# Graph transformer layer on 4096 nodes: the first q and all of k made once for all heads and placed by DMA, the next tile's q at step 11, VectorE's LayerNorm 2 in eight parts

## The reference

```python
qkv = layer_norm(x, g1, be1) @ w_qkv                  # (N, 3, 8, 16)
scores = jnp.einsum('nhd,mhd->hnm', q, k) * SCALE
scores = jnp.where(mask, scores, -jnp.inf)            # mask = adj != 0, for all heads
attn = jax.nn.softmax(scores, axis=-1)
out = jnp.einsum('hnm,mhd->nhd', attn, v).reshape(n, DIM)
x = x + out @ w_proj + b_proj
h2 = layer_norm(x, g2, be2)
return x + gelu(h2 @ w1 + b1) @ w2 + b2
```

## Time and profile before

| | us |
|---|---|
| median of 3 runs | 1702.24 |
| lowest and highest | 1699.94, 1702.98 |
| the profiled execution | 1704.14 |
| its span | 1702.3 |

### The profile page before, as it was taken

How to read it: one execution, slowest core, us unless ns; L and a number is a source line. 1 busy time by engine, 2 the same in 40 slices (tenths; PEclk the granted TensorE clock), 3 DMA queues, 4 the chain that set the end, 5 groups by cost and what they waited for, 6 DMA issues and landing times.

```text
span 1702.3 us, 46524 instructions
## 1 busy us (share of the span) xinstructions
PE 1588.7 (93%) x17016; PEld 496.5 (29%) x17016; DVE 1419.3 (83%) x4490; ACT 1274.2 (75%) x1394; POOL 1167.4 (69%) x1092
## 2 busy tenths in 40 slices
PE   6989999999999999999999999999999999999996
PEld 3422222323223232232323232232323232232323
DVE  6888989987999889997898879998899879988811
ACT  4647878777777878778776877778787787868793
POOL 4955487569865798568875698567885688657551
PEclk9979999999999999999999999999999999999997
DMA  8810046301460046500462025700464015600000
GB/s 214 184 52 2 5 142 128 76 5 57 141 124 30 5 116 138 97 5 26 137 127 63 5 81 136 134 2 5 133 130 88 4 39 148 123 18 5 14 5 13
DMA packets 177856, 125.88 MB, mean 74 GB/s; under 512 B 140974, under 2 KB 155183, under 8 KB 177628
## 3 DMA queue, kind: packets, MB, share of 16 engines
q1 hardware_dynamic: 163196, 108.49, 26.7%
q10 hardware_dynamic: 14432, 14.42, 3.3%
HBM read 77.25 MB, written 6.04 MB: 49 GB/s over the span
## 4 chain that ended last, share of the span: by engine, by line
PE 52%; ACT 22%; issue 14%; POOL 8%; DVE 2%; ACTq 1%; DMA 1%; SPq 0%; POOLq 0%; DVEq 0%
ACT probs L820 20%; PE pv_ps L1149 15%; PE ring_ps L1080 10%; PE score_ps L1241 9%; PE score_ps L1256 9%; POOL probs L582 2%; PE ring_ps L1207 2%; PE score_ps L1173 2%; POOL k_stack L543 2%; ACT q_stack L689 1%; DVE masked_out L858 1%; PE ring_ps L1198 1%; PE ring_ps L1183 1%; PE ring_ps L1190 1%; POOL row_mask L517 1%
## 5 line engine op out<-in xcount | busy, mean ns | idle before, releaser
L858 DVE CUSTOM_DVE_ANT_0 masked_out<-ring_ps,row_mask 128x512 bf16<-128x512 f32 x2048 | 1311.9, 688 | 138.6 <-PE ring_ps L1080 99.3
L820 ACT ACTIVATE probs<-score_ps,score_scale 128x1024 f32<-128x1024 f32 x1010 | 1075.6, 1112 | 338.5 <-PE score_ps L1256 324.4
L582 POOL TENSOR_TENSOR probs<-probs,keep 128x1024 int32<-128x1024 int32 x256 | 604.2, 2361 | 252.1 <-ACT probs L820 241.6
L1149 PE MATMUL pv_ps<-probs,v_ones 128*17 128x512 f32 x4096 | 543.7, 599 | 4.6 <-POOL probs L582 4.0
L1080 PE MATMUL ring_ps<-k_stack,q_stack 51*64 51x512 f16 x4096 | 488.0, 397 | 15.1 <-DVE row_max L858 13.8
L1256 PE MATMUL score_ps<-q_stack,k_stack 51*64 51x512 f16 x4040 | 370.4, 391 | 18.9
L1080 PEld LDWEIGHTS ring_ps<-k_stack,q_stack 51*64 51x64 f16 x4096 | 169.0, 104 | 495.7 <-DVE row_max L858 446.2
L1241 PE MATMUL score_ps<-mask_t,ident_bf 64*64 64x512 bf16 x3028 | 274.9, 387 | 34.1 <-ACT probs L820 15.5
L1256 PEld LDWEIGHTS score_ps<-q_stack,k_stack 51*64 51x64 f16 x4040 | 115.6, 104 | 211.6 <-PE score_ps L1241 183.6
L858 DVE DVE_READ_ACCUMULATOR2_ANT row_max<- 128x1 f32 x2048 | 169.9, 83 | 0.0
L521 POOL TENSOR_SCALAR row_mask<-row_mask 128x1024 bf16<-128x1024 bf16 x124 | 129.5, 1045 | 23.6 <-POOL row_mask L517 23.0
(11 more groups left out here) (128 smaller groups left out, 840.3 us busy)
## 6 DMA issues: line engine op xcount, KB each, us to landing
adj_in<-adj SPq DMA_DIRECT2D x128, 512.0 KB, 4.2
halves<-attn ACTq DMA_DIRECT2D x30, 128.0 KB, 2.7
q_stack<-q_dram SPq DMA_DIRECT2D x42, 64.0 KB
mask_t<-row_mask SPq DMA_TRANSPOSE x128, 3.5
xq<-xnT_dram ACTq DMA_DIRECT2D x8, 256.0 KB, 2.7
halves<-halves ACTq DMA_DIRECT2D x16, 128.0 KB, 2.2
x_res<-x ACTq DMA_DIRECT2D x8, 256.0 KB, 4.5
out<-rows ACTq DMA_DIRECT2D x8, 256.0 KB, 5.4
```

What stands on the lines that cost most here:

```text
L582: nc.gpsimd.tensor_tensor(view, view, keep[:, KEPT.index(m), :].unsqueeze(1).broadcast_to([128, 2, TILE]), ALU.mult).then_inc(probs_masked, 1)
L820: nc.scalar.activation(probs[:, (2 * g + n) % SLOTS, :], score_banks(i, place).rearrange("p a n -> p (a n)"), ACT.Exp, scale=score_scale[: ...
L858: nc.vector.tensor_tensor_reduce(out=masked_out[:, place % 3, :], in0=ring_ps[:, place % 3, :], in1=row_mask[:, j, ch * 512:(ch + 1) * 512 ...
L1149: last = nc.tensor.matmul(pv_ps[32 * k:32 * k + HD + 1, :], v_ones[:, block_of(g, b), 2 * p + a, :], probs[:, (2 * g + b) % SLOTS, a * TIL ...
```

## The change

Three things change.

**The opening's items.** There are 9 items (`ITEMS = 1 + CHUNKS`): one for the first q and one for each chunk of k, each for all heads with the plain weight (`wq_all`, `wk_all`). ScalarE copies an item as f16 and as f32 (`take_item`), GpSimd subtracts them into the low part, ScalarE stores both parts to `item_dram` (`store_item`), and when they have landed places them: six loads for q, nine for each chunk of k (`load_item`). The replicated weights and `part_coef` go. The shift unit of k_stack is set by VectorE and spread by two DMAs. The row units run 8 steps behind instead of 7, and wait for the loads. GpSimd converts two mask pieces after each item from 1 to 6.

**q at step 11.** The fill moves from step 33, GpSimd's subtraction to step 12. SyncE stores and places q before the next tile's mask loads instead of among them.

**LayerNorm 2.** VectorE's four parts become eight, behind the second and the fourth row maximum of steps 9 to 12.

```diff
-ACT_FILLS = {H2T_STEP: ("h2t",), 33: ("q",)}
+Q_MADE = 11
+ACT_FILLS = {H2T_STEP: ("h2t",), Q_MADE: ("q",)}
-Q_STEP = 34
+Q_STEP = Q_MADE + 1
-ITEMS = PAIRS * (1 + CHUNKS)
+FIRST_PER = 4
+ITEMS = 1 + CHUNKS
-ROW_LAG = 7
+ROW_LAG = 8
-POOL_FIRST_MASKS = {4 + 2 * k: 4 + k for k in range(CONVERTED - 4)}
+POOL_FIRST_MASKS = {n: (2 * n + 2, 2 * n + 3) for n in range(1, 7)}
@@ SyncE, a tile
+                store_q(i, par)
+                load_q(i, par)
                 for k in range(CONVERTED):
                     sp.wait_ge(flag_done, (i + 1) * CONVERTED + (k - 5))
                     load_adj((i + 1) * SUB + k // ADJ_C, k % ADJ_C, k % 2)
-                    if k == Q_STORE_LOAD:
-                        store_q(i, par)
-                    if k == Q_STORE_LOAD + 1:
-                        load_q(i, par)
@@ GpSimd, the opening
-                nc.gpsimd.tensor_tensor(dst, item_x[n % DEPTH], item_neg[n % DEPTH], ALU.add).then_inc(item_done, 1)
+                nc.gpsimd.tensor_tensor(item_part[n % DEPTH][1], item_x[n % DEPTH], item_part[n % DEPTH][0],
+                                        ALU.subtract).then_inc(item_done, 1)
@@ ScalarE, the opening
+            def take_item(n):
+                act.wait_ge(item_full, n + 1)
+                if n >= DEPTH:
+                    act.wait_ge(item_stored[n - DEPTH], 32)
+                nc.scalar.copy(item_part[n % DEPTH][0], score_ps[:, n % 4, :])
+                nc.scalar.copy(item_x[n % DEPTH], score_ps[:, n % 4, :]).then_inc(item_read, 1)
+            def store_item(n):
+                act.wait_ge(item_done, n + 1)
+                for low in range(2):
+                    act.dma_start(item_dram[n, low], item_part[n % DEPTH][low]).then_inc(item_stored[n], 16)
+            def load_item(n):
+                act.wait_ge(item_stored[n], 32)
+                for m, first in enumerate(PART_ROW):
+                    low = Q_LOW[m] if n == 0 else K_LOW[m]
+                    heads = item_dram[n, low].rearrange("(p a d) n -> a d p n", a=2, d=HD)
+                    for a in range(2):
+                        rows = slice(HALF * a + first, HALF * a + first + HD)
+                        to = q_stack[0][rows, :, :] if n == 0 else k_stack[rows, :, n - 1, K_FIRST:]
+                        act.dma_start(to, heads[a]).then_inc(item_in[n], 16)
+                    if n > 0:
+                        act.dma_start(k_stack[rows, :, n - 1, 0:K_FIRST],
+                                      heads[1][:, :, 128 * 2 + 64:128 * 3]).then_inc(item_in[n], 16)
+            for c in range(CHUNKS):
+                transposed_rows(c)
+                if c == 1:
+                    load_item(0)
+                if c >= 1:
+                    load_item(c)
+                if c + 1 < CHUNKS:
+                    root(c + 1)
+                if c == 0:
+                    take_item(0)
+                take_item(c + 1)
+                act.wait_ge(stage_full, 2 * c + 2)
+                nc.scalar.copy(v_ones[:, c * SUB:(c + 1) * SUB, :, 0:HD],
+                               pv_ps[:, :].rearrange("p (s h d) -> p s h d", s=SUB, h=HEADS)).then_inc(v_done, 1)
+                if c == 0:
+                    store_item(0)
+                store_item(c + 1)
+            load_item(CHUNKS)
@@ TensorE, the opening
+                    if j == 0:
+                        pe.wait_ge(item_in[ch + 1], 16 * (3 * len(PART_ROW)))
@@ VectorE, LayerNorm 2
-                        if x == 1 and d and LN2_STEP <= g < LN2_STEP + 4:
-                            layer_norm2(i, bcd, g - LN2_STEP)
+                        if x % 2 == 1 and d and LN2_STEP <= g < LN2_STEP + 4:
+                            layer_norm2(i, bcd, 2 * (g - LN2_STEP) + x // 2)
```

More of the change, by code:

```diff
@@ L252, in program @@
         zero_dram = nc.dram_tensor("zero_dram", (SHIFT_PARTS + 1, PAIRS, TILE), F16, kind="Internal").ap()
+        item_dram = nc.dram_tensor("item_dram", (ITEMS, 2, DIM, 512), F16, kind="Internal").ap()
         q_dram = nc.dram_tensor("q_dram", (2, 2, DIM, TILE), F16, kind="Internal").ap()
@@ L328, in program @@
         item_full, item_read, item_done = sem("item_full"), sem("item_read"), sem("item_done")
+        item_stored, item_in = ([sem(f"item_stored{n}") for n in range(ITEMS)], [sem(f"item_in{n}") for n in range(ITEMS)])
+        unit_in = sem("unit_in")
         shift_full, shift_stored = sem("shift_full"), sem("shift_stored")
@@ L706, in _ @@
+            act.wait_ge(unit_set, 2)
+            for a in range(2):
+                own = k_stack[HALF * a + SHIFT_ROW:HALF * a + SHIFT_ROW + SHIFT_PARTS + 1, :, :, :]\
+                    .rearrange("r p c k -> r (p c) k")
+                act.dma_start(own[:, 1:, :], own[:, 0:1, :].broadcast_to([SHIFT_PARTS + 1, PAIRS * CHUNKS - 1, K_CHUNK]))\
+                  .then_inc(unit_in, 16)
             root(0)
-            act.wait_ge(q_clear, 2)
+            act.wait_ge(q_clear, 4)
             act.wait_ge(w_in, 16 * 5)
-            act.wait_ge(consts_in, 16 * 4)
+            act.wait_ge(consts_in, 16 * 3)
@@ L979, in layer_norm2 @@
                 before = (i - 1) * LN2_STEPS
[L980 to L985 removed]
+                if k < SUB:
+                    dve.wait_ge(row_taken, made(ROWS, i, bcd, DVE_PLACE[PROJ_STEP + k // 2]))
+                    nc.vector.bn_stats(stats[:, k, :], x_res[:, k, :]).then_inc(ln2_step, 1)
+                elif k < SUB + 2:
                     dve.wait_ge(ln2_step, before + SUB)
[L987 removed]
+                    for s in range(2 * (k - SUB), 2 * (k - SUB) + 2):
                         nc.vector.bn_aggr(mean_var[:, s, :], stats[:, s, :]).then_inc(ln2_step, 1)
[L989 removed]
+                elif k == SUB + 2:
                     dve.wait_ge(ln2_step, before + 2 * SUB)
@@ L1289, in constants @@
 def constants():
-    c = np.zeros((128, 136), np.float32)
+    c = np.zeros((128, 132), np.float32)
     c[:, 0:128] = np.eye(128)
@@ L1293, in constants @@
         c[32 * k + HD, 128 + k] = 1.0
-    for r in range(128):
-        for n, first in enumerate(PART_ROW):
-            if first <= r % HALF < first + HD:
-                c[r, 132] = -Q_LOW[n]
-                c[r, 133] = -K_LOW[n]
-        if SHIFT_ROW <= r % HALF < SHIFT_ROW + SHIFT_PARTS:
-            c[r, 135] = SHIFT_UNIT
     return c
```

103 lines of the change are left out of this document (33 added, 70 removed).

## The result

| | before | after |
|---|---|---|
| median of the runs, us | 1702.05 (4 runs) | 1725.37 (4 runs, 1723.67 to 1726.86) |
| ratio, 95% interval | | 1.0138, 1.0121 to 1.0156 |
| span of the profiled execution | 1702.3 | 1725.0 |
| first exponential of the main loop | 119.6 | 149.1 |
| from there to the end | 1582.7 | 1575.8 |

The kernel is 23.3 us slower where +9.4 was forecast. The loss is in the opening, +29.5 us; the tiles give 6.9 back, near the forecast 6.3.

What follows compares the result with a forecast made beforehand. It took GpSimd and TensorE to bound the opening, then VectorE's row maxima, and TensorE the tiles except steps 9 to 13 (VectorE). +15.7 - 5.3 - 1.0 = +9.4 us gave 1711.6 us, range 1697 to 1726.

Steps and rivals of the forecast that it cites:

- The sign: Whole kernel: forecast slower, +9.4 us; slower by over 0.2% was given 0.69.
- the tiles' sum: Eight main-loop tiles: q at step 11 and the finer LayerNorm 2 together take off 6.3 us.
- the opening's term: Opening: the DRAM chain puts the last item in place at 114.6 instead of 98.89 us, +15.7 us.
- the start: Opening: xnT's store issued by 27.3 us, then fifteen loads taking 6.7, so first loads done at 34.0 us.
- the period: Opening, per chunk: ScalarE's chain of 7.4 us plus a 3.8 us landing gives 11.2 us, against 10.2 before.
- rival 3: Opening: the DMA engines become the bound, landings 5.7 us, period 13.1, opening +29, time 1725 us; chance 0.12.
- rival 1: Opening: item stores land in 2.2 us, period 9.6, opening +4.5, time 1700.4 us, no change; chance 0.17.
- The tail: Opening's end: after the last item 28 row units remain at VectorE's pace, 18.8 us as before.
- q at step 11: Tiles two to seven: saves 1.28 us at step 33, costs 0.4 at step 11; -0.9 a tile, -5.3 us.
- Rival 4: Tiles: q costs at step 11 what it cost at 33, step 11 longer by 1.1 or more; 1717 us; chance 0.10.
- LayerNorm 2 in eight parts: Seven tiles, steps 9 to 12: finer parts gain between 0 and 0.4 a tile, taken as 0.15; -1.0 us.
- The clock: Opening: TensorE's granted clock share, 0.91 then 0.61 before, might change with less work; an unpriced cost.

Runs made afterwards that it cites:

- unit_pool: The changed kernel with GpSimd setting all of k_stack to the shift unit in one memset, without the two spreading DMAs; 1721.95 us.
- light_masks: The changed kernel with the opening's last twelve mask loads reading 256 instead of 1024 columns, so masks are wrong; 1718.29 us.
- ln8_only: The kernel before with only VectorE's LayerNorm 2 in eight parts; 1697.58 us, ratio 0.9979.
- opening_only: The changed kernel with q back at step 33 and LayerNorm 2 in four parts; 1729.89 us, ratio 1.0172 to the kernel before.
- warm_after: The changed kernel with six extra matmuls a chunk in the opening, never read, to hold TensorE's clock up; 1725.74 us.
- light_root_first: The changed kernel with quarter-column first-tile mask loads, and the root and next item's copies ahead of the item's loads; 1717.49 us.
- few_loads: unit_pool with three instead of nine loads for each k chunk, so scores are wrong; 1711.38 us.
- light_root_warm1: light_root_first with three more unread matmuls a chunk on TensorE; 1715.10 us.
- unit_late: The changed kernel with the two spreading DMAs issued only before the first loads, in ScalarE's second chunk; 1729.83 us.
- root_first: The changed kernel with ScalarE's square root and next item's copies ahead of the nine loads instead of behind them; 1727.22 us.

## Why the prediction was wrong, by its steps

**The sign and the tiles' sum held, the opening's term failed**: +15.7 forecast, +29.25 measured at the last chunk. Of the 13.5 us between them 8.1 are the start and 5.5 the seven periods. Two steps failed: the start, where the spreading DMAs and the wait for the first stores were put at nothing, and the period, whose landings and issues were priced as if the sixteen DMA engines were no fuller than before. The time, 1725.4, lies at the upper end of the range and at what rival 3 gave.

**The start**: 34.0 forecast, 42.1 measured. Three parts make the 8.1. ScalarE had issued xnT's store at 27.3 by the forecast and at 31.99 in the trace, 4.7 later: the two spreading DMAs, which have no term in the sum, delay the mask loads, 5.1 us at the fourth mask, and unit_pool takes 4.1 us back. Then the queue waits for the first items' stores, 1.6 us before q's loads and 1.1 before k's, where the sum had no wait. Last, the fifteen loads take 7.4 us to issue instead of 6.7.

**The period**: 11.2 forecast, 12.0 measured. As a mean the chain was priced well: the times from the last store's issue to the first load are 8.5, 2.0, 4.2, 6.0, 2.0, 2.6 and 1.9 us, mean 3.9, where 3.8 was taken. Off were the nine loads, 4.1 to 5.9 us, mean 4.8, against 4.03: 0.8 a period, which is nearly all of the excess. But the mean is partly luck: the four periods with the DMA share at 1.07 are 13.5 us, 2.3 over the forecast, and the three with it at 0.50 are 9.9, 1.3 under. light_masks, with 11.0 us in those four, shows that the load on the DMA engines makes most of it. Rival 3 named this, and its 13.1 is close to the 13.5, but it took it for all seven periods.

The size that kept rival 3 at 0.12 was wrong. It put the added DMA work at 2.0 us a chunk, from 265 GB/s in a stretch "of such rows", but of that stretch's bytes the greater part is in 4 KB packets (108, with 77 of 1 KB). A 1 KB packet took 49 ns there, and 82.0 ns on ScalarE's queue in the opening of the kernel after. The queue's rows show 21.6 us added by six items, q's and five of k, 3.6 each: 7.8 + 3.6 = 11.4 us a chunk instead of 9.8, more than the forecast period of 11.2. The argument against the rival, that a longer period lowers the share again, needs the work to be less than the period. The rival's own 1725 is right partly by two errors: 13.1 for all seven periods is 7.7 us too much in all, and its start 8.1 too early.

**Short landings.** By the fit of the Trainium skill (DMA: Bandwidth & Descriptors, "Anatomy of one DMA — SWDGE (gpsimd) path") 128 KB take 2.3 us, an estimate from that page, which gives the fit for DMAs that GpSimd issues; these are ScalarE's. The shortest landing here, 1.7, is under it, the median of 4.1 is nearly twice it. Where landings are short, another chain shows that the sum left out: root, LayerNorm, transposes, xnT's copy and store, and then the loads. The last three periods are 10.2, 9.8 and 9.9, not the 9.4 that the sum gives with its shortest landing. So rival 1's 9.6 was not quite reached even with them.

**The tail** was right, 19.0 for 18.8.

**q at step 11.** The 1.28 at step 33 is right to the hundredth. At step 11 it costs 0.89 and at step 12 another 0.03, not 0.4 in all, so -0.9 a tile became -0.36 (-2.2 in six tiles), and alone only -0.14. Rival 4's bound was 1.1; the truth lies nearer to it than to the forecast. The 5.7 us of TensorE's waits were read as room. But 5.4 us of them are still there with q beside them. They are waits for VectorE within the ring; that q can fill only one in which it stands itself is a reading that no run tests.

**LayerNorm 2 in eight parts.** Forecast -0.15 a tile with a bound of 0.4; alone it gives 0.39, the bound. "A gain can only come from a burst longer than the ring's cover" was wrong as a limit: none was over 1 us, and cutting them gained all the same. That each delays the row maxima behind it is the likely cause, and not shown. The two errors in the tiles cancel in part. Steps 10, 11 and 33 make 3.9 of the 6.9 us; the other 3.0 are small differences, mostly at steps 3, 24, 34 and 35, whose cause wasn't looked for. ln8_only has those at 3 and 35 too, and opening_only, with neither part, those at 24, 34 and 35, so much of this is not the two parts' gain.

**The clock**, named as what could break it outright, fell indeed: 0.50 from 23.3 to 163.2 us. It did not set the 12.0 us: warm_after has 12.2 with most of the clock back. With the DMA engines relieved and the root first, most of it back is worth 1.3 us a chunk, after the cost of the three matmuls.

What stays open: whether the full DMA engines hold the four long periods by their throughput or by the landings that they lengthen in the chain, since every run that took work away shortened both; and what the number of small packets does, since no run changed packet size alone.

## What to carry to other kernels

Before a copy made by an engine is replaced by DMAs, add the DMA work of the stage to the DMA share that it has already: price the new packets by rows of their own size and queue, with room for doubt (a 1 KB packet took 49 ns in one stretch and 82.0 in the full one). If the DMA work of a chunk comes near its period, expect that work or the longer landings to set the period, however cheap each issue is. A loop of store, landing and load on one queue shouldn't have the next chunk's root behind it, but before the root is moved ahead, follow what then waits for the loads: here it was TensorE, and through it the next copies. A short instruction series beside a ring of banks can be worth cutting finer than its length suggests: here it gained 0.39 us a tile.

## What the runs showed of the hardware

- **Three periods close together.** 12.0 us a chunk in the kernel after (13.5 while the DMA share is 1.07), 10.8 with light masks and the root first at TensorE's 1.2 GHz, 9.5 there with it near 2.4 GHz. Taking one limit away shows only the next: light_root_first is no faster than light_masks. The 10.8 is that order's pace and no floor of the clock: the last three periods of the kernel after are 10.2, 9.8 and 9.9 at the same 0.50.
- **Less TensorE work, half the clock.** Busy 68.7 of 73.9 us, the kernel before had 0.91; busy 47.4 us, the kernel after had 0.50. The busy time alone doesn't tell it: few_loads had 0.50 while busy 35.9 of 38.9 us. From light_root_first to light_root_warm1 three more matmuls a chunk brought 0.96 for 0.50 and a shorter period.
- **A small DMA delays the loads of another queue.** The two spreading DMAs, 2.15 us of issue on ScalarE's queue and 186 packets of 1152 bytes from 7.0 to 16.2 us, held VectorE's second mask, which SyncE's queue loads, until 22.20 us (16.91 in unit_late, where they come later).
- **Landings vary with the load.** The same 128 KB stores landed in 1.7 us at the least and 8.5 at the most; in root_first TensorE waited until 7.8 us after the last issue of k's loads, with the DMA share at 1.17 in those 7.8 us.
- **The clock's record can be missing.** root_first's profile shows 1.00 through the opening, but its row matmuls of 51x512 take 631 ns as in the kernel after, where the clock is 0.50; in light_root_warm1, at 0.96, they take 415. The mean duration of a known matmul is the safer reading.
